# Routed experts block by block: shares multiplied into y, higher rows scattered into the output, the rest added by accumulating transfers

## What is computed

```python
x = x + xattn(_layernorm(x), ctx)      # softmax of q k^T mixes the rows of the normalised x
xf = _layernorm(x).reshape(-1, 256)    # 1024 tokens
ew, ei = top_k(xf @ gate_w.T, 2)
ew = softmax(ew)                       # the shares of the two experts
x1 = silu(einsum('td,ehd->teh', xf, w_gate)); x3 = einsum('td,ehd->teh', xf, w_up)
expert_out = einsum('teh,edh->ted', x1 * x3, w_down)
routed = sum over the two experts of ew * expert_out
shared = silu(xf @ sh_gate.T) * (xf @ sh_up.T) @ sh_down.T
x = x + routed + sigmoid(xf @ se_gate_w.T) * shared
```

## Time and profile before

| | us |
|---|---|
| median of 3 runs | 107.85 |
| lowest, highest | 105.22, 108.12 |
| the profiled execution: its time | 105.32 |
| the profiled execution: its span | 103.5 |
| TensorE busy | 85.5 (83%) |
| VectorE busy | 62.1 (60%) |
| ScalarE busy | 46.5 (45%) |
| GpSimd busy | 44.8 (43%) |
| mean granted TensorE clock | 0.947 |

### The profile page before, as it was taken

The page is one execution under the profiler, slowest core; times in us unless marked ns, Lnnn a source line. Parts: engine busy times, 40 slices in busy tenths (PEclk is TensorE's granted clock), DMA queues, the critical chain, the costliest instruction groups (busy, mean ns, idle before and its releaser), DMA issues.

```text
span 103.5 us, 1864 instructions
## 1 busy us (share of the span) xinstructions
PE 85.5 (83%) x514; PEld 68.5 (66%) x514; DVE 62.1 (60%) x274; ACT 46.5 (45%) x104; POOL 44.8 (43%) x60
## 2 busy tenths in 40 slices
PE   6799999997999999996799999999999989600000
PEld 2386789895974478443789999999999968400000
DVE  1188989999999889202986444566444320604990
ACT  0556657758685991433036454466454361000000
POOL 7012002388676777300000567668667677710000
PEclk9999999999999999999999999999999999985555
DMA  2975999992232222256163434655412212059946
GB/s 20 376 267 133 410 413 401 333 348 77 93 108 104 104 104 104 104 142 177 26 186 104 112 107 134 188 152 161 154 46 100 96 56 101 0 90 355 369 180 225
DMA packets 10586, 17.50 MB, mean 169 GB/s; under 512 B 1613, under 2 KB 6095, under 8 KB 10576
## 3 DMA queue, kind: packets, MB, share of 16 engines
q1 hardware_dynamic: 7264, 10.63, 32.7%
q0 software_dynamic: 1872, 4.27, 11.2%
q10 hardware_dynamic: 1440, 2.49, 6.6%
HBM read 10.85 MB, written 7.44 MB: 177 GB/s over the span
## 4 chain that ended last, share of the span: by engine, by line
PE 64%; DMA 12%; DVE 12%; issue 3%; DVEq 3%; POOLq 1%; POOL 1%; ACT 1%; ACTq 0%
PE bank L1064 20%; PE bank L998 12%; PE bank L1079 9%; DMA upper_y<-routed_dram 6%; PE bank L1048 4%; DMA proj_sb<-proj 4%; PE bank L942 4%; PE bank L1034 4%; PE bank L898 3%; PE bank L923 3%; DVEq L285 2%; DMA routed_dram<-y_sb,place 2%; PE bank L906 2%; DVE x L642 2%; PE bank L907 2%
## 5 line engine op out<-in xcount | busy, mean ns | idle before, releaser
L365 POOL DMA_INDIRECT routed_dram<-y_sb,place x23 | 23.6, 1025 | 25.0 <-DVE place L780 15.4
L1064 PEld LDWEIGHTS bank<-xgT,hidden_w 128*128 128x128 f32 x184 | 22.4, 192 | 2.3 <-issue 1.8
L1064 PE MATMUL bank<-xgT,hidden_w 128*128 128x128 f32 x184 | 22.6, 275 | 1.1 <-DVE hidden_w L798 1.1
L352 POOL DMA_INDIRECT slots_dram<-rows,slot x16 | 15.7, 981 | 6.8 <-issue 4.4
L998 PE MATMUL bank<-xnT,ffn_sb 128*128 128x512 f32 (+1 forms) x36 | 14.6, 550 | 0.0
L806 DVE TENSOR_TENSOR r_act<-bank,r_silu 128x256 f32<-128x256 f32 (+1 forms) x12 | 5.0, 414 | 15.9 <-ACT r_silu L514 14.2
L1079 PE MATMUL bank<-ffn_sb,r_act 128*128 x46 | 12.0, 382 | 0.3 <-ACT y_sb L526 0.3
L514 ACT ACTIVATE r_silu<-bank 128x256 f32<-128x256 f32 (+1 forms) x12 | 4.5, 376 | 15.3 <-PE bank L1064 15.3
L998 PEld LDWEIGHTS bank<-xnT,ffn_sb 128*128 128x128 f32 x36 | 6.6, 190 | 5.5 <-issue 5.3
L798 DVE COPY hidden_w<-ffn_sb 128x512 f32 x23 | 8.7, 419 | 1.9 <-issue 1.9
L1079 PEld LDWEIGHTS bank<-ffn_sb,r_act 128*128 128x128 f32 x46 | 7.8, 190 | 1.2 <-issue 0.7
(11 more groups left out here) (119 smaller groups left out, 128.9 us busy)
## 6 DMA issues: line engine op xcount, KB each, us to landing
ffn_sb<-ffn SPq DMA_DIRECT2D x2, 1536.0 KB, 9.6
xg<-slots_dram SPq DMA_DIRECT2D x23, 132.0 KB, 2.2
slots_dram<-empty SPq DMA_DIRECT2D x1, 1056.0 KB, 14.2
x_sb<-x ACTq DMA_DIRECT2D x4, 256.0 KB, 5.0
ffn_sb<-ffn SPq DMA_DIRECT2D x1, 768.0 KB, 4.3
lower_y<-routed_dram SPq DMA_DIRECT2D x2, 256.0 KB, 4.2
lower_y<-routed_dram ACTq DMA_DIRECT2D x2, 256.0 KB, 4.5
upper_y<-routed_dram SPq DMA_DIRECT2D x2, 256.0 KB, 5.6
```

What stands on the lines that cost most here:

```text
L352: pool.indirect_dma_start(out=slots_dram[:, :], out_offset=bass.IndirectOffsetOnAxis(ap=slot[:, i, a:a + 1], axis=0), in_=rows[:, i, :], i ...
L365: pool.indirect_dma_start(out=routed_dram[0:planes * TOKENS, :], out_offset=bass.IndirectOffsetOnAxis(ap=place[:, j:j + 1], axis=0), in_=y ...
L1064: last = pe.matmul(hidden_of(p, kind)[:, j % 2, :], hidden_w[:, j % NW, c:c + P], xgT[:, p % 2, k, j % 2, :], start=(k == 0), stop=(k == K ...
```

## The change

The loops of the routed stage run over single blocks j = 0..22 on every engine, with y in six one-block buffers and the PSUM banks dealt out anew: the hidden products go to banks 4 and 5, y to banks 6 and 2.

The share is multiplied into y by `store_y` as it leaves PSUM (`scale=share`). For that each scattered row carries two more columns, the first choice's number and the scaled difference of the two scores, written in `slots(b)` by three small instructions for each batch; per block VectorE computes `half` (plus or minus a half), ScalarE a tanh (`lean_of`), VectorE the share (`share_of`). The computation of all shares at once (`routed_shares`, two instructions of `margins`) goes.

The output gets two planes. Rows of the higher expert are scattered straight into plane 0, which is the result, and rows of the lower into plane 1, which the host drops. At the end only plane 1 is loaded, `add_lower` adds it to `x1` with a plain addition, and four transfers on GpSimd's queue add `x1` to plane 0 in DRAM (`accum_op=ALU.add`), once all scattered rows have landed.

At the start of the stage VectorE reads the expert numbers and stages the weights before `shared_act(1, 0)`, and TensorE does `shared_up(1, 0)` before `shared_gate(1, 1)`.

```diff
-NY = 3
+NY = 6
...
-        GU_BANK = [bank[1], bank[2]]
-        Y_BANK = [bank[6], bank[3]]
+        GU_BANK = [bank[4], bank[5]]
+        Y_BANK = [bank[6], bank[2]]
...
+        def hidden_of(j, kind):
+
+            return GU_BANK[j % 2][:, kind * P:(kind + 1) * P]
...
-                    sp.wait_ge(xgT_ready, (j - NXG) // 2 + 1)
-                    sp.wait_ge(place_ready, (j - NXG) // 2 + 1)
+                    sp.wait_ge(xgT_ready, j - NXG + 1)
+                    sp.wait_ge(place_ready, j - NXG + 1)
+                    sp.wait_ge(lean_ready, j - NXG + 1)
...
-            wait_for_upper(sp)
-            load_upper(sp, 0)
-            load_upper(sp, 2)
-            store_out(sp, 0)
-            store_out(sp, 2)
-            store_out(sp, 3, 1, 2)
-            sp.wait_ge(out_stored, 16 * (B + 1))
+            sp.wait_ge(out_stored, 16 * STORES)
...
             def send_y(j):
-                p, k = j // 2, j % 2
-                if p >= SINGLE:
-                    pool.wait_ge(y_stored, j + 1)
-                elif k == 0:
-                    pool.wait_ge(y_stored, 2 * p + 2)
-                if k == 0:
-                    pool.wait_ge(place_ready, p + 1)
+                pool.wait_ge(y_stored, j + 1)
+                pool.wait_ge(place_ready, j + 1)
                 planes = 1 if j == LAST else 2
                 pool.indirect_dma_start(
-                    out=routed_dram[0:planes * TOKENS, :],
-                    out_offset=bass.IndirectOffsetOnAxis(ap=place[:, j:j + 1], axis=0), in_=y_sb[:, p % NY, k, :],
-                    in_offset=None, bounds_check=planes * TOKENS - 1, oob_is_err=False).then_inc(y_sent[p % NY], 16)
+                    out=planes_of[0:planes * TOKENS, :],
+                    out_offset=bass.IndirectOffsetOnAxis(ap=place[:, j:j + 1], axis=0), in_=y_sb[:, j % NY, :],
+                    in_offset=None, bounds_check=planes * TOKENS - 1, oob_is_err=False).then_inc(y_sent[j % NY], 16)
+
+            def add_to_out(k):
+
+                t = tiles_of(k, STORES)
+                pool.wait_ge(out_ready, t.stop)
+                pool.dma_start(out_tiles(0, t), x1[:, t, :], accum_op=ALU.add).then_inc(out_stored, 16)
 
...
+            for i in range(NY):
+                pool.wait_ge(y_sent[i], 16 * rows_sent(i))
+            for k in range(STORES):
+                add_to_out(k)
...
+            def store_xgT(j):
+                act.wait_ge(xgT_ready, j + 1)
+                if j >= 2:
+                    act.wait_ge(gu_ready, j - 1)
+                act.copy(xgT[:, j % 2], XG_BANK[j % 2][:, 0:KT * P].rearrange(
+                    "p (k n) -> p k n", k=KT)).then_inc(xgT_stored, 1)
+
+            def routed_silu(j):
+                act.wait_ge(gu_ready, j + 1)
+                if j >= 2:
+                    act.wait_ge(r_act_ready, j - 1)
+                act.activation(r_silu[:, j % 2, :], hidden_of(j, 0), ACT.Silu).then_inc(r_silu_ready, 1)
+
+            def store_y(j):
+                act.wait_ge(y_ready, j + 1)
+                if j >= NY:
+                    act.wait_ge(y_sent[j % NY], 16 * (j // NY))
+                act.wait_ge(share_ready, j + 1)
+                act.activation(y_sb[:, j % NY, :], y_of(j), ACT.Copy, scale=share[:, j:j + 1]).then_inc(y_stored, 1)
+
+            def lean_of(j):
+                act.wait_ge(half_ready, j + 1)
+                act.activation(lean[:, j:j + 1], xg[:, j % NXG, L + 3:L + 4], ACT.Tanh,
+                               scale=half[:, j:j + 1]).then_inc(lean_ready, 1)
...
-            for p in range(PAIRS):
-                routed_silu(p)
-                if p + 2 < PAIRS:
-                    store_xgT(p + 2)
-                if p >= 1:
-                    store_y(p - 1)
-            store_y(PAIRS - 1)
+            for j in range(BLOCKS):
+                routed_silu(j)
+                if j + 2 < BLOCKS:
+                    store_xgT(j + 2)
+                lean_of(j)
+                if j >= 1:
+                    store_y(j - 1)
+            store_y(BLOCKS - 1)
...
-                then(dve.tensor_tensor(margin[:, :, 0], top[:, :, 0], top[:, :, 1], ALU.subtract))
-                dve.tensor_tensor(margin[:, :, 0], margin[:, :, 0], rstd2[:], ALU.mult)
-                dve.tensor_tensor(margin[:, :, 1], score[:, :, E], rstd2[:], ALU.mult).then_inc(margin_ready, 1)
+                dve.tensor_tensor(margin[:], score[:, :, E], rstd2[:], ALU.mult).then_inc(margin_ready, 1)
...
+                dve.tensor_copy(rows[:, both, L + 2], topi[:, both, 0])
+                for i in range(b * LT, (b + 1) * LT):
+                    dve.scalar_tensor_tensor(rows[:, i, L + 3:L + 4], top[:, i, 1:2], top[:, i, 0:1], rstd2[:, i:i + 1],
+                                             ALU.subtract, ALU.mult)
                 dve.wait_ge(prefix_ready, b + 1)
...
+            def places(j):
+
+                dve.wait_ge(xg_in[j % NXG], 16 * (j // NXG + 1))
+                dve.tensor_scalar(plane[:, j:j + 1], xg[:, j % NXG, L + 1:L + 2], expert[:, j:j + 1], float(TOKENS),
+                                  ALU.is_equal, ALU.mult).then_inc(plane_ready, 1)
+
+                dve.tensor_scalar(half[:, j:j + 1], xg[:, j % NXG, L + 2:L + 3], expert[:, j:j + 1], 0.5,
+                                  ALU.not_equal, ALU.subtract).then_inc(half_ready, 1)
+                dve.wait_ge(plane_ready, j + 1)
+                dve.tensor_tensor(place[:, j:j + 1], plane[:, j:j + 1], xg[:, j % NXG, L:L + 1].bitcast(I32),
+                                  ALU.add).then_inc(place_ready, 1)
+
+            def share_of(j):
+                dve.wait_ge(lean_ready, j + 1)
+                dve.tensor_scalar(share[:, j:j + 1], lean[:, j:j + 1], 0.5, 0.5, ALU.mult,
+                                  ALU.add).then_inc(share_ready, 1)
 
...
             def add_lower(i):
                 dve.wait_ge(lower_in[i * LOWS // NT], 16)
-                dve.scalar_tensor_tensor(x1[:, i, :], lower_y[:, i, :], share_lower[:, i:i + 1], x1[:, i, :],
-                                         ALU.mult, ALU.add).then_inc(lower_added, 1)
-
-            def add_upper(i):
-                dve.wait_ge(lower_added, i + 1)
-                dve.wait_ge(upper_in[i * UPS // NT], 16)
-                dve.scalar_tensor_tensor(x1[:, i, :], upper_y[:, i, :], share_upper[:, i:i + 1], x1[:, i, :],
-                                         ALU.mult, ALU.add).then_inc(out_ready, 1)
+                dve.tensor_tensor(x1[:, i, :], lower_y[:, i, :], x1[:, i, :], ALU.add).then_inc(out_ready, 1)
...
             base(0)
-            shared_act(1, 0)
             experts()
             stage(0)
+            stage(1)
+            shared_act(1, 0)
+            stage(2)
             places(0)
-            stage(1)
-            places(1)
-            routed_shares()
-            for p in range(PAIRS):
-                routed_act(p)
-                if p + 2 < PAIRS:
-                    stage(p + 2)
-                    places(p + 2)
-                if p == 0:
+            for j in range(BLOCKS):
+                routed_act(j)
+                if j + 3 < BLOCKS:
+                    stage(j + 3)
+                if j == 0:
                     shared_act(1, 1)
+                share_of(j)
+                if j + 1 < BLOCKS:
+                    places(j + 1)
             base(1)
             dve.wait_ge(base_ready, 2)
             for i in range(NT):
                 add_lower(i)
-            for i in range(NT):
-                add_upper(i)
...
+            def routed_hidden(j):
+                if j >= 2:
+                    pe.wait_ge(r_act_ready, j - 1)
+                pe.wait_ge(xgT_stored, j + 1)
+                pe.wait_ge(staged, j + 1)
...
+                    pe.wait_ge(y_stored, j - 1)
+                pe.wait_ge(r_act_ready, j + 1)
+                u = bass.ds(chosen[j], 1)
+                pe.matmul(y_of(j), r_act[:, j % 2, :], ffn_sb[:, u, 2 * L:3 * L].rearrange("p o n -> p (o n)"),
+                          start=True, stop=True).then_inc(y_ready, 1)
...
             shared_gate(1, 0)
+            shared_up(1, 0)
             shared_gate(1, 1)
-            shared_up(1, 0)
...
-    out = nc.dram_tensor("out", (B, P, LT * L), F32, kind="ExternalOutput").ap()
+    out = nc.dram_tensor("out", (2, P, NT * L), F32, kind="ExternalOutput").ap()
...
-    return np.ascontiguousarray(result.reshape(B, L, L))
+    return np.ascontiguousarray(result[0].reshape(P, B, LT, L).transpose(1, 0, 2, 3).reshape(B, L, L))
```

More of the change, by code:

```diff
@@ L131, in xattn_moe_kernel @@
         plane = sb("plane", [P, JB])
+        half = sb("half", [P, JB])
+        lean = sb("lean", [P, JB])
+        share = sb("share", [P, JB])
         place = sb("place", [P, JB], I32)
@@ L259, in upper_rows, with tiles_of, out_tiles @@
-        def upper_rows(k):
-            return slice(k * NT // UPS, (k + 1) * NT // UPS)
+        planes_of = out.rearrange("a p (i n) -> (a p i) n", n=L)
+        def tiles_of(k, parts):
```

(30 more changed lines are left out.)

184 lines of the change are left out of this document (51 added, 133 removed).

## The result

Four runs of the changed kernel took 106.5 to 107.6 us, median 107.3; the kernel before took 105.22 to 108.12 us in four, median 106.55. Two of the four runs of the kernel before, 107.85 and 108.12 us, were slow ones, and the ratio leaves them out: 1.019 (95% interval 1.011 to 1.026), where the two medians alone would give 1.007. The profiled executions are 107.6 us after (span 105.8) and 105.32 before (span 103.5).

The account below looks back on a forecast made before the run. TensorE paces the routed stage, with start and end uncovered. Start 0.4 us earlier after shrinking, lower load 3.1 earlier, accumulation landing at 100.4: span 100.5 against 103.5; 3.0 off the 107.85 median gives 104.8 us, range 101.3 to 108.1.

Parts of the forecast that it names:

- The start: Start of routed stage: weights staged earlier give 2.05 us, three added instructions per batch cost 1.0; hidden products from 48.8.
- The stage: Routed stage: TensorE stays the pace at 1.545 us a block; ScalarE, VectorE and GpSimd all stay under that.
- Rival 2: Routed stage: exchanges between ScalarE and VectorE break the pace, 1.80 us a block, net 2.6 us slower, median 110.4; chance 0.13.
- The scatters: End of routed stage: GpSimd is never behind, last scatter at 86.8, lower load at 87.7, 3.1 us earlier.
- Rival 3: Routed stage: VectorE's staging copies lock out GpSimd's scatters, 1.71 us each, scatter gain gone, median 108; chance 0.04.
- the last term of the tail: Last accumulating transfer, start to landing: 3.4 us, from 1.0 issuing, 2.0 plain store, 0.4 reading old values.
- the high end of 6.36: Tail: upper bound for the last accumulating transfer's start to landing, taken from a 256 KB load among eight.
- Rival 1: Tail: accumulating transfers land like upper loads, 6.36 us after the last start; span 103.5, no change, median 107.8; chance 0.15.
- signs of being wrong: TensorE waiting for xgT or r_act, accumulating transfers over 5 us, or GpSimd needing much over 1.3 us to issue one.

Follow-up runs that it names:

- no_columns_b: two_loads without the three small routing instructions of each batch on VectorE, measured beside a repeat of two_loads: 101.64 us, ratio 0.964 to the kernel before.
- acc_sbuf: Changed kernel, lower plane accumulated into x1 in SBUF by four transfers, x1 plainly stored by SyncE and ScalarE, higher rows left out: 105.43 us.
- plain_pool: Changed kernel with its four last transfers as plain stores on GpSimd's queue, higher experts' rows not added: 103.31 us, ratio 0.976 to the kernel before.
- parts1: Changed kernel with one accumulating transfer of 1 MB in place of four of 256 KB: span 105.9 us.
- parts8: Changed kernel with eight accumulating transfers of 128 KB in place of four of 256 KB: span 105.8 us.
- start_only: Kernel before with only the register load and first staging moved ahead of the shared expert's product on VectorE: 104.47 us, ratio 0.986.
- split_adds: two_loads with GpSimd doing both additions of the last two of eight tiles: ratio 0.982 to the kernel before.
- two_loads: Changed kernel with both planes loaded, added plainly and stored on SyncE's and ScalarE's queues: 102.36 us, again 102.19, ratio 0.968 to the kernel before.
- plain_hw: Changed kernel with four plain stores on SyncE's and ScalarE's queues, higher experts' rows not added: 99.75 and 101.74 us, no ratio.

## Why the prediction was wrong

Right, point by point. **The start**: forecast 2.05 - 1.0 us. Counted from the first attention addition, the hidden products began after 34.69 us before, 33.49 after (1.2 gained), and 32.59 in no_columns_b (2.1). Both terms hold. In the profile the changed kernel shows 49.25 and not 48.8 because its first addition came at 15.76, 0.6 later, ahead of the routing and the routed stage; in the traces here it lies anywhere from 15.0 to 17.0. **The stage**: 1.54 us a block, without a gap; y with a scale took 0.47 as taken, the tanh with a scale 0.30 instead of 0.20, and VectorE had half a microsecond to spare before each product. Rival 2 is refuted. **The scatters**: 0.98 to 1.0 us each, though a staging copy ran beside them (each scatter starts some 0.1 us before the copy, where the one of 1.09 us had started inside one), the last at 87.60 (forecast 86.8), the lower load at 88.61 (87.7), the first accumulating transfer at 93.86 (93.1); the differences are that 0.6 and 0.2 to 0.3 of small hand-overs. Rival 3 is refuted.

Wrong was the last term of the tail: "The cost from start to landing of the last one is not in the trace ... I take 3.4", and with it the high end of 6.36. It measured 8.1: 3.4 was forecast for the time from the last transfer's start to its landing, and this term is 4.7 us too small. The step that failed is that I priced the last of four transfers by itself, as issuing plus a store plus "0.4 for reading the old values, near the low end since few transfers are in flight". All four were in flight together: a part of 256 KB keeps the DMA engines busy for a quarter of 7.5 us, 1.9, GpSimd starts one each 0.6 (93.9 to 95.6), and so the last one waits for the three before it. The pace that I did check, GpSimd's issuing at 1.3 us, was not the slow one. The sum for the whole megabyte, 9.9 us from the first issue, should have stood in the place of the last part's. The term "0.4 for reading the old values" stands on no row; the adding costs 7.5 - 2.9 = 4.6 us of engine time for the megabyte, over 1.1 for each part.

A second term was missing altogether: the program's end waits for GpSimd's drain, 1.7 us after the landing. The trace of before had that drain, hidden under the loads (from 87.1 to 94.2, 3.25 us behind the end of its last scatter instruction at 90.93), and I did not look at it. Together: the landing was forecast at 100.4; add 0.8 for the later first transfer, take off 2.2 for quicker issuing, add 4.7 for the landing, and it comes at 103.7, as measured; 1.8 for the drain, which ended at 105.6, and 0.2 to the program's end give the span.

Rival 1 had the right mechanism and too low a price: its 6.36 from rows of before would have meant no change; 8.1 was measured, and the drain was not in it either. Its argument against ("they come one by one") is what the runs reversed. Of the signs of being wrong that the prediction named, one came: the accumulating transfers took over 5 us.

One thing was luck. The forecast of 104.8 subtracts 3.0 us from a median of 107.85, while the trace that it was worked out on took 105.32, and in three of the four later comparisons the kernel before had medians of 105.6 to 105.8. That the measured 107.3 lies between 101.3 and 108.1 is owed to that high base: taken from 105.32, the forecast was 102.3.

Of the price, the runs show that it goes mostly by bytes and in part by pieces (1, 4 and 8 transfers), hardly by where the destination lies (acc_sbuf), and that the DMA engines are fully busy at it. The rate, 123 to 182 GB/s in full stretches with four transfers against 377 for the plain stores, is a third to a half. The Trainium skill, "Collectives: The Full Stack", section "The bandwidth ceiling", has the second source read on the same ring halve the rate. The trace with one transfer agrees (5.8 us of busy engines against 2.9 for plain stores); with four and eight transfers the cost was 2.6 and 3.1 times the plain one. My use of it, one part of 256 KB taken twice as long, was the same mistake as in the sum. That it is the second read, and not the addition itself, was not tried.

## What to carry to other kernels

A transfer that adds is no free addition: here a megabyte took 9.9 us from the first issue to the last landing, where plain stores from the same queue took 4.8 and eight vector additions take 2.8, and it replaced work (a load and additions) that lay mostly beside other work. Price the last stage as a whole, all bytes in flight over the rate at which they move, not its last transfer alone. And see which queue ends the program: move the last stores (and the last additions) off GpSimd, whose drain comes after them, and keep the share in y and the loop by blocks, which gave 3.2% once the accumulation was gone.

## What the runs showed that I had not expected

GpSimd's drain at the program's end has two lengths. Where its last transfers landed late, it ended 1.7 to 2.0 us after the last landing (after, plain_pool, parts1, parts8, acc_sbuf). Otherwise it ended 3.25 to 3.3 us after GpSimd's last instruction or last wait (before, start_only, split_adds, two_loads, plain_hw). In each of these runs that is the later of the two moments.

GpSimd's instruction itself takes longer for an accumulating transfer, 0.97 to 1.86 us for 256 KB, than for a plain one, 0.54 to 0.60. But the records overlap: both kinds start about 0.6 us apart (93.9 to 95.6 and 95.2 to 96.8 for four).

```profile
L334 POOL DMA_DIRECT2D out<-x x4: 539/555/598, 95.2 to 96.8; - x4
```

A scale from SBUF made the 128x1 tanh 0.30 us, where the same size without one took 0.20.
